# Graph network with four residual norms: factors' bias product at full height, and another order around the gated state

## The reference

```
h = relu(bn1(conv1(x)));  x_conv = relu(bn2(conv2(h, 17 taps)) + x)
s = x @ w_se.T + b_se                      # three factors per node
dist[n, m] = |s_n|^2 + |s_m|^2 - 2 s_n . s_m
A = exp(-dist) * mask;  x_nmp = A @ relu(x @ w_msg.T + b_msg)
r, z = sigmoid(...);  n = tanh(gi_n + r * gh_n);  y = (1 - z) * n + z * x
```

## Time and profile before

| | us |
|---|---|
| median of 3 runs | 765.79 (764.44 to 767.04) |
| the profiled execution, its own time | 766.93 |
| span from its first to its last instruction | 765.1 |
| TensorE busy | 704.0 (92%) |
| VectorE busy | 621.8 (81%) |
| ScalarE busy | 422.9 (55%) |
| GpSimd busy | 131.3 (17%) |
| mean granted TensorE clock, share of full speed | 0.977 |

### The profile page before, as it was taken

One profiled execution on the slowest core, in us unless ns is written; L12 is line 12 of the kernel. 1 busy time (PEld: TensorE's weight loads), 2 busy tenths in 40 slices (PEclk: granted clock), 3 DMA queues, 4 the chain that ended last, 5 costly groups with the idle time before them and its releaser, 6 DMA issues.

```text
span 765.1 us, 12798 instructions
## 1 busy us (share of the span) xinstructions
PE 704.0 (92%) x3968; PEld 544.0 (71%) x3968; DVE 621.8 (81%) x2081; ACT 422.9 (55%) x883; POOL 131.3 (17%) x151
## 2 busy tenths in 40 slices
PE   4879999999999999999999999999999999998653
PEld 3666868777787877777786877778687777775541
DVE  7556788889888888889888888988888888976765
ACT  4353736657384655647374665738465564734351
POOL 0000111212121221212121121212122121211221
PEclk9999999999999999999999999999999999998787
DMA  5306041331605133250604233060513325101000
GB/s 203 124 7 226 17 152 69 124 126 28 220 15 178 55 132 115 77 170 14 211 36 151 82 123 124 23 224 14 178 55 127 120 71 176 56 12 59 0 15 28
DMA packets 46445, 75.26 MB, mean 98 GB/s; under 512 B 4050, under 2 KB 12628, under 8 KB 46292
## 3 DMA queue, kind: packets, MB, share of 16 engines
q1 hardware_dynamic: 46420, 74.96, 29.0%
HBM read 70.76 MB, written 4.19 MB: 98 GB/s over the span
## 4 chain that ended last, share of the span: by engine, by line
PE 62%; DVE 20%; ACT 8%; issue 6%; POOL 4%; DVEq 0%; ACTq 0%; POOLq 0%
PE C L1429 7%; PE F L1437 7%; PE K L1466 7%; PE K L1332 6%; PE F L1359 6%; PE K L1301 5%; PE CONV L1332 4%; PE C L1359 3%; PE C L1301 3%; POOL RSTD L367 3%; ACT X L427 2%; PE K L1320 2%; PE K L1475 2%; DVE X L717 2%; DVE Z L1032 2%
## 5 line engine op out<-in xcount | busy, mean ns | idle before, releaser
L348 POOL TENSOR_TENSOR RSTD<-VEPS,POW 128x4 f32<-128x4 f32 x48 | 49.2, 1024 | 293.1 <-DVE VEPS L711 293.1
L1332 PE MATMUL CONV<-H1H,WH 128*128 128x256 f32 x288 | 83.3, 289 | 2.9 <-DVE H1L L729 2.9
L1332 PE MATMUL CONV<-H1L,WH 128*128 128x256 f32 x288 | 81.9, 284 | 0.0
L1332 PE MATMUL CONV<-H1H,WL 128*128 128x256 f32 x288 | 81.5, 283 | 0.0
L1429 PE MATMUL C<-QT,KT 128*128 128x512 f32 x128 | 60.9, 616 | 4.1 <-DVE KT L869 3.4
L1301 PEld LDWEIGHTS K<-XS,BIG 128*128 128x128 f32 x496 | 59.4, 196 | 3.9 <-DVE XS L998 2.5
L1301 PE MATMUL K<-XS,BIG 128*128 128x128 f32 x496 | 59.8, 280 | 2.5 <-DVE XS L998 2.5
L1437 PE MATMUL F<-A,MSG 128*128 128x512 f32 x128 | 57.6, 593 | 1.1 <-issue 1.1
L1332 PEld LDWEIGHTS CONV<-H1H,WH 128*128 128x128 f32 x288 | 55.3, 192 | 4.5 <-ACT H L436 3.6
L1332 PEld LDWEIGHTS CONV<-H1L,WH 128*128 128x128 f32 x288 | 55.3, 192 | 0.7
L1332 PEld LDWEIGHTS CONV<-H1H,WL 128*128 128x128 f32 x288 | 55.5, 193 | 0.0
(11 more groups left out here) (273 smaller groups left out, 1946.2 us busy)
## 6 DMA issues: line engine op xcount, KB each, us to landing
ADJF<-in_adjT SPq DMA_DIRECT2D x16, 1024.0 KB, 5.3
ADJN<-in_adj SPq DMA_DIRECT2D x16, 1024.0 KB, 7.7
ADJM<-in_adjT SPq DMA_DIRECT2D x15, 1024.0 KB, 5.5
ADJR<-in_adjT SPq DMA_DIRECT2D x14, 1024.0 KB, 5.3
X_IN<-in_xT SPq DMA_DIRECT2D x16, 256.0 KB, 2.6
out<-OUT SPq DMA_DIRECT2D x16, 256.0 KB, 2.8
BIG<-in_weights SPq DMA_DIRECT2D x1, 1088.0 KB, 5.4
BIG<-in_weights SPq DMA_DIRECT2D x1, 576.0 KB, 8.7
```

What stands on the lines that cost most here:

```text
L348: nc.gpsimd.tensor_tensor(RSTD[:, row, :], VEPS[:, row, :], POW[:, 0, :], ALU.pow).then_inc(ev[f"ln{layer}_rstd"], 1)
L1332: last = mm(out, w[:, at_col + k * P:at_col + (k + 1) * P], h[:, k:k + PH], start=(k == 0 and i == 0), stop=(k == count - 1 and i == 2))
```

## The change

The bias product of `factors` gets 128 rows: SE, SEZ, SEH and ONER grow from 2 to 128 partitions, with zeros in rows 2 to 127 of the bias, so that the transfer of SE is 64 KB in place of 1 KB. It now comes last of the four, behind the three products of x. On ScalarE `parts` goes ahead of `update_gate`, and `first_conv` moves into the next slot, behind the tanh of `new_state` and ahead of the table load. On VectorE `stacked` is split: STL comes right behind `reset`, then `new_input`, `kept_state`, `gated`, and only then STR and `rest_of_h1`. On TensorE slot 1 now has the transposes and distances ahead of `first_taps`, as the later slots have.

```
-        SE = sb("SE", [2, P])
-        SEZ, SEH = sb("SEZ", [2, P], F32R), sb("SEH", [2, P], F32R)
-        ONER = sb("ONER", [2, N], F32R)
+        SE = sb("SE", [P, P])
+        SEZ, SEH = sb("SEZ", [P, P], F32R), sb("SEH", [P, P], F32R)
+        ONER = sb("ONER", [P, N], F32R)
...
                 if mid:
                     new_state(n)
+                    first_conv(n["f"], n["f_prev"])
                 nc.scalar.preload_act_table_set("natural_log_exp_and_others")
...
                 if following:
                     squares(n["f_next"])
-                    first_conv(n["f_next"], n["f"])
+                    parts(n["f_next"])
                 update_gate(n)
-                if following:
-                    parts(n["f_next"])
...
-            V.tensor_scalar(SEZ[:, :], SE[:, :], PAR[0:2, SE_LEFT:SE_LEFT + 1], None, ALU.mult).then_inc(s_se, 1)
+            V.tensor_scalar(SEZ[:, :], SE[:, :], PAR[:, SE_LEFT:SE_LEFT + 1], None, ALU.mult).then_inc(s_se, 1)
...
-            def stacked(count):
+            def stacked_left(count):
                 dve.wait_ge(ev["zr_ready"], count)
                 V.scalar_tensor_tensor(STL[:, :], K0[:, :], PAR[:, L_A:L_A + 1], ZL[:, :].bitcast(F32),
                                        ALU.mult, ALU.subtract)
+
+            def stacked_right(count):
+                dve.wait_ge(ev["zr_ready"], count)
                 V.scalar_tensor_tensor(STR[:, :], K0[:, :], PAR[:, R_A:R_A + 1], ZR[:, :].bitcast(F32),
                                        ALU.mult, ALU.subtract).then_inc(ev["str_ready"], 1)
...
                 reset(n)
                 if following:
-                    rest_of_h1(n["f_next"], n["f"])
+                    stacked_left(n["f_next"])
+                new_input(n)
                 if following:
                     kept_state(n["f"])
-                new_input(n)
-                if following:
-                    stacked(n["f_next"])
                     gated(n["f"])
+                    stacked_right(n["f_next"])
+                    rest_of_h1(n["f_next"], n["f"])
...
-                mm(K0[:, :], SEH[:, :], ONER[:, :], start=True, stop=False)
                 for k, (w, x) in enumerate(((WH, XH), (WH, XL), (WL, XH))):
-                    last = mm(K0[:, :], w[:, W_SE:W_SE + P], x[:, :], start=False, stop=(k == 2))
+                    mm(K0[:, :], w[:, W_SE:W_SE + P], x[:, :], start=(k == 0), stop=False)
+                last = mm(K0[:, :], SEH[:, :], ONER[:, :], start=False, stop=True)
                 last.then_inc(ev["g1_done"], 1)
...
-                starting = isinstance(t, int) and t < 2
+                starting = isinstance(t, int) and t < 1
...
-    se = zeros((2, P), np.float32)
+    se = zeros((P, P), np.float32)
     for at_col in (0, 3, 6, *range(32, 44, 3)):
-        se[:, at_col:at_col + 3] = i["L0_gnn_b_se"]
+        se[0:2, at_col:at_col + 3] = i["L0_gnn_b_se"]
```

More of the change, by code:

```diff
@@ L599, in ending @@
                 new_state(a)
+                first_conv(a["f"], a["f_prev"])
                 nc.scalar.preload_act_table_set("natural_log_exp_and_others")
@@ L760, in _ @@
             rest_of_h1(1, 0)
-            stacked(1)
+            stacked_left(1)
+            stacked_right(1)
             split(S_ODD, less_odd, 5)
```

## The result

The changed kernel took 746.92 us (median of 4 runs, 746.82 to 747.34) against 765.53 for the kernel before (4 runs, 764.44 to 767.04). The ratio is 0.976, with a 95% interval of 0.9746 to 0.9774: faster by 18.6 us, where 16.8 us and a time of 749.0 were forecast. The profiled execution took 746.84 us against 766.93, which is 20.1 us less; its span is 745.1.

A forecast was written before the change was run, and what follows sets the result against it. TensorE, busy 92% of the span, was taken as the bound, with its wait for Y to close. 15 borders of 1.10 us (16.5) and the prologue made 16.8 us, giving a median of 749.0, range 746.0 to 756.0.

The forecast's parts named there:

- The wait for Y: TensorE at each slot's opening: a repeated wait, 0.61 us by the idle figure, which the new order would remove.
- The new order: At a border, tile times worked out from measured steps: Y 1.55 us earlier, transposes 1.13 earlier, ST 1.10 earlier.
- The gap: TensorE between `attended` and the transposes of Y: 0.77 us from start to start, to be closed at each border.
- The bias: `factors` on TensorE: changing from 128 rows to 2 and back costs 0.36 us, saved with 128 rows throughout.
- ST and its 0.03 us: VectorE's statistics, queued behind H1L: ST starts 1.10 us earlier, 0.03 less than TensorE's gain.
- The covers: At a border, time to spare before each is needed: STR 0.2 us, H1L 0.6, table load 0.2.
- Rival 2: At borders, a new wait (STR, table load or loop's branch) overruns by 0.3 to 0.6 us: 754 to 758; chance 0.13.
- The table load: ScalarE, now behind H1: runs 389.57 to 390.85, while the exps need it at 391.07.
- the case for an unchanged time: ScalarE's table load adds 1.38 us of drain, exps start as late as now, time near 766; chance 0.02.
- rival 3: ScalarE's queue, longer between tanh and table load, becomes the bound; two extra loads give 784 us; chance 0.04.
- Prologue: Before the slots: even steps save 0.58 us, the larger bias transfer takes half, leaving 0.3.
- Slot 1: Transposes ahead of the taps: Y 1.6 us earlier, norm 1.1 earlier; a lower clock could cost up to 1.

The follow-up runs named there:

- experiment 2: The changed kernel with the bias product as before (2 rows, first of the four), all new orders kept: 754.78 us, ratio 0.985.
- experiment 6: The changed kernel with ScalarE's queue as before and VectorE's order new: 778.92 us, ratio 1.0171 against the kernel before.
- 7: The changed kernel with VectorE's order as before except H1L, which stays last: 759.73 us, ratio 0.9906 against the kernel before.
- 1: The kernel before with only the bias product changed (128 rows, last of the four), all orders as before: 759.37 us, ratio 0.9917.
- 3: The changed kernel with 2 rows in the bias record, still last of the four: 753.11 us, ratio 0.9849 against the kernel before.
- 4: The changed kernel with 65 rows in the bias record in place of 128: 746.1 us, ratio 0.9747 against the kernel before.
- 5: The changed kernel with 64 rows in the bias record in place of 128: 754.4 us, ratio 0.9842 against the kernel before.
- experiment 9: The changed kernel with one more ScalarE activation, an unread copy behind the relus and ahead of the table load: 747.22 us, ratio 0.9749.

## Why the prediction was right, point by point

- **The wait for Y as the thing to close: right.** Without it the slots are 0.85 us shorter (experiment 2), and where it comes back (6 and 7) the time comes back too.
- **The new order, tile by tile: right.** Set to the same clock (10.07 us between the two starts of `attended`, after the 0.36 of the bias), the trace has GT at 386.80, the tanh at 387.51, NG at 388.26, Y at 388.99, STR at 389.60, H1L at 390.26 and ST at 390.86. The prediction had 386.77, 387.49, 388.25, 388.97, 389.58, 390.24 and 390.86.
- **The gap: 0.77 predicted, 0.78 measured** (4.34 to 3.56 us behind `attended`). A further 0.06 was not in the sum: from the first transpose to the attention the changed kernel takes 11.90 us, the one before 11.96. The transposes and the first distance product are closer together when they follow other products (380.06 to 380.42, where the earlier trace rows have 391.27 to 391.68).
- **The bias: 0.36 predicted, 0.39 measured** (experiments 1, 3, 4 and 5). My sum took 0.24 for a plain step of 0.233 and stopped one step early.
- **ST and its 0.03 us: priced, but free.** ST starts 0.73 behind the transposes in place of 0.69, and KT is not later for it: before, VectorE stood for 0.1 us further on, until TensorE's products for its tile MSG were there, and that pause is gone. So a border gives 0.39 + 0.78 + 0.06 = 1.23 where I had 1.10, and the ledger has 1.20 to 1.24. Over 14 borders that is 1.9 us.
- **The covers.** Predicted 0.2 us for STR, 0.6 for H1L, 0.2 for the table load; measured 0.15, 0.58 and 0.14. Experiment 9 overran the last by 0.36 for nothing. Rival 2 feared for the right place but took a start that comes late for a slot that gets longer; the wait for KT behind it was the real cover.
- **The loop's branches: nothing, as taken.** The loop's borders gained 1.24 us each, the two written-out ones ahead of them 1.2.
- **The table load: right.** It starts 0.02 us after H1's end, lasts 1.28, and experiment 9 has the next activation 0.01 after its end. No drain is seen, so the case for an unchanged time fell.
- **The other side.** ScalarE's queue does turn the change into a loss, but by another way than rival 3: not by its length behind the tanh, but by the place of ZR ahead of it (experiment 6, +12.6 us).
- **Prologue: half right.** The long steps went (the four products of `factors` and those after it run in even steps), but the larger transfer holds the constants back by 0.46 us (SEZ at 4.99, before at 4.53). The first taps are 0.11 earlier, where 0.3 was taken.
- **Slot 1: the ledger's 1.34 us meet the forecast of 1.4 (a border and the prologue) by luck.** Y was expected 1.6 us earlier and came 3.2 earlier, since TensorE's clock stayed at 2.4 GHz during the gates, where it had fallen to 1.2 for the steps from 39.8 to 42.8 us before. It was then at 1.2 GHz from 46.9 to 50.3 us, behind the 3.0 us wait and into the taps. Other traces with the same slot 1 differ: with 65 rows, after the same wait, the clock did not fall and the attention began at 57.61; in the second trace of the changed kernel it was low for 6.8 us and the attention began at 59.95. So how much of the 1.34 is the change stays open. That the edit was needed for H1L I had missed.
- **The tail: not in the sum, and mostly not the change.** 1.43 us of the ledger lie behind the attention of slot 15. Of these, 0.28 go with ScalarE's order: from that attention to the last transposes it takes 28.38 us in the three traces with the old order (before, 1, 6) and 28.10 in the other eleven. The rest goes with the granted clock. Over the fourteen traces the stretch takes 96.9 to 99.7 us: up to 97.2 in the four where its mean granted clock is 0.87, 98.0 to 98.5 in the four with 0.85, 98.5 to 99.5 in the four with 0.83 to 0.84, and 99.5 to 99.7 in the two with 0.82. The trace before is of the third kind, the one after of the second. Why the clock differs is not known. This and slot 1 are why whole times repeat less well than slots.
- **The total.** The profiled execution got 20.1 us shorter, not 16.8: 1.9 more at the borders and 1.4 more in the tail. The median came 2.1 below 749.0. The path was right and its borders were priced 0.13 us too low; the tail was no part of the forecast.

## What to carry to other kernels

When an engine's queue is full but for one repeated wait, work out at that wait where every tile that stands ahead of the awaited one is first needed; those needed later go behind it, but the engines that feed them must be reordered in the same step, and any place that uses the old order (here slot 1) with them. Price a wait from start to start, against a place in the trace where it doesn't occur, not by the idle figure. A small operand between full ones can cost more than a padded one; here 65 rows were enough. Compare kernels by the slots in which the granted clock is the same, since the stretches outside them differed by up to 3 us between traces here, along with the clock.

## What the runs showed of the hardware

- A product with 2 or 64 rows between products with 128 lengthens the three steps around it from 0.233 us each to 0.33, 0.43 and 0.33 to 0.34, together 0.39 to 0.40 us per record (experiments 1, 3 and 5). With 65 rows, as with 128, all steps are plain. That the array is set for 128 rows or for fewer, by whether the record has more than 64, and that changing back and forth costs time on both sides, fits these steps but is inferred from them: heights other than 2, 64, 65 and 128 were not run.
- A table load on ScalarE starts 0.02 us behind the activation before it, takes 1.28 us, and the next activation starts 0.01 us behind it (experiment 9).
- One and the same wait did not always go with the same clock. After the wait of 3.0 us in slot 1 the clock fell to 1.2 GHz for 3.4 us in the first trace of the changed kernel and not at all in the trace with 65 rows; in the second trace of the changed kernel it had fallen 0.9 us before that wait ended, and was low for 6.8 us.
